# Two-stage attention block on one core: new order in the last head, loads before the last stores, and an output projection on four quarters of TensorE

## The reference

```
x = x + window_attention(group_norm(x))      # 49-pixel windows, 16 heads of 16, softmax
# second stage, on the result x1
n  = group_norm(x1)
p  = 25 shifted copies of n (5 x 5 neighbourhood, zeros outside)     # per pixel
q  = n
s  = sum over the 8 channels of a head of p * q                      # 8 heads, 25 scores per pixel
a  = softmax(s over the 25 shifts)
o  = sum over the 25 shifts of p * a                                 # 64 channels
out = x1 + w_out @ o + b_out                                         # w_out is 64 x 64
```

## Time and profile before

| | us |
|---|---|
| median of the runs | 1789.05 |
| the profiled execution, its time | 1798.7 |
| its span | 1797.0 |
| VectorE busy | 1434.3 (80%) |
| TensorE busy | 1435.7 (80%) |
| GpSimd busy | 1187.3 (66%) |
| ScalarE busy | 1051.5 (59%) |

### The profile page before, as it was taken

How to read it: one execution, slowest core, us unless ns; L and a number is a source line. 1 busy time by engine, 2 the same in 40 slices (tenths; PEclk the granted TensorE clock), 3 DMA queues, 4 the chain that set the end, 5 groups by cost and what they waited for, 6 DMA issues and landing times.

```text
span 1797.0 us, 60281 instructions
## 1 busy us (share of the span) xinstructions
PE 1435.7 (80%) x25001; PEld 704.2 (39%) x25001; DVE 1434.3 (80%) x1975; ACT 1051.5 (59%) x1883; POOL 1187.3 (66%) x860
## 2 busy tenths in 40 slices
PE   4999999999999999936887869777786876867745
PEld 2656666666666666610222212212221221213322
DVE  4776777777777777769999998999989899995924
ACT  3446777777777777735555747466574656543300
POOL 5334555555555555500999899999999999995700
PEclk9568999999999999956898998999999899997868
DMA  8702010202015101060225133252312422026079
GB/s 334 278 11 55 18 54 18 54 18 54 18 49 87 54 18 54 18 165 7 56 51 128 29 75 78 50 129 51 88 49 59 115 51 67 22 68 247 21 289 390
DMA packets 106860, 156.12 MB, mean 87 GB/s; under 512 B 71362, under 2 KB 83650, under 8 KB 100034
## 3 DMA queue, kind: packets, MB, share of 16 engines
q1 hardware_dynamic: 106690, 153.60, 29.2%
HBM read 81.92 MB, written 65.20 MB: 82 GB/s over the span
## 4 chain that ended last, share of the span: by engine, by line
PE 39%; POOL 27%; DVE 16%; issue 12%; ACT 2%; SPq 1%; DMA 1%; DVEq 0%; POOLq 0%
POOL arena L800 20%; PE PS L1312 6%; PE PS L1471 5%; PE PS L1321 5%; PE PS L1337 5%; POOL arena L811 4%; DVE arena L1104 4%; PE PS L1289 4%; DVE arena L1100 4%; PE PS L1281 4%; PE PS L1494 3%; PE PS L1300 2%; PE PS L1351 2%; DVE arena L1211 2%; PE PS L1419 2%
## 5 line engine op out<-in xcount | busy, mean ns | idle before, releaser
L800 POOL TENSOR_TENSOR arena<-arena 128x2016 f32<-128x2016 f32 (+2 forms) x168 | 604.9, 3635 | 78.9 <-PE PS L1419 78.7
L1211 DVE TENSOR_TENSOR arena<-arena,PS 128x1568 f32<-128x1568 f32 x348 | 610.3, 1778 | 39.6 <-PE PS L1471 32.6
L766 POOL TENSOR_TENSOR arena<-arena,consts 128x196 f32<-128x196 f32 x512 | 294.3, 608 | 278.1 <-ACT arena L850 278.1
L1471 PE MATMUL PS<-arena,consts 32*32 32x392 f32 x12800 | 391.3, 513 | 83.8 <-DVE arena L1211 46.9
L992 ACT ACTIVATE PS<-arena 128x392 f32<-128x392 f32 x348 | 172.9, 499 | 271.4 <-DVE arena L1211 269.5
L1419 PE MATMUL PS<-arena,consts 128*32 128x504 f32 (+2 forms) x1664 | 225.6, 618 | 119.9 <-POOL arena L800 76.7
L1471 PEld LDWEIGHTS PS<-arena,consts 32*32 32x32 f32 x12800 | 140.2, 104 | 337.4 <-DVE arena L1211 179.1
L1100 DVE TENSOR_REDUCE arena<-PS 128x8 f32<-128x392 f32 x256 | 143.3, 560 | 142.3 <-PE PS L1312 140.9
L875 ACT ACTIVATE arena<-PS 128x512 f32<-128x512 f32 x256 | 153.0, 598 | 155.0 <-PE PS L1321 151.6
L811 POOL TENSOR_TENSOR arena<-arena 128x1568 f32<-128x1568 f32 x52 | 159.3, 3076 | 49.0 <-ACT arena L938 21.6
L1321 PE MATMUL PS<-consts,arena 128*128 128x128 f32 x1024 | 176.6, 297 | 0.2
(11 more groups left out here) (105 smaller groups left out, 1670.6 us busy)
## 6 DMA issues: line engine op xcount, KB each, us to landing
arena<-x_wide_dram SPq DMA_DIRECT2D x256, 82.5 KB, 2.1
arena<-x_wide_dram SPq DMA_DIRECT2D x32, 660.0 KB, 8.3
x_wide_dram<-arena SPq DMA_DIRECT2D x12, 1125.0 KB
arena<-in_x_dram SPq DMA_DIRECT2D x8, 1568.0 KB, 15.2
x_wide_dram<-arena SPq DMA_DIRECT2D x64, 196.0 KB, 4.4
x_dram<-arena SPq DMA_DIRECT2D x8, 1568.0 KB, 7.4
attn_dram<-arena SPq DMA_DIRECT2D x256, 49.0 KB, 2.9
arena<-x_dram SPq DMA_DIRECT2D x8, 1568.0 KB, 18.9
```

What stands on the lines that cost most here:

```text
L766: i = nc.gpsimd.tensor_tensor(k_bd[k][:, r], keys.unsqueeze(1).to_broadcast([P, HEADS_T, S]), head_mask.unsqueeze(2).to_broadcast([P, HEAD ...
L800: nc.gpsimd.tensor_tensor(tile, x_part, by, ALU.mult).then_inc(pool_tile, 1)
L1211: nc.vector.tensor_tensor(by_channel(v_tiles[n % V_RING]), shifted_values(half, k), over_channels(PS[:, 2 + n % W_BANKS, 0:PIX]), ALU.mult ...
L1471: mm = nc.tensor.matmul(PS[dst, 4 + i, 0:PIX], ident[src, src], tile[src, c * PIX:(c + 1) * PIX], start=done == 0, stop=done == NK - 1)
```

## The change: what it does

1. `RECIPROCAL_LAST`: in the last head VectorE's reciprocal stands before the last 12 of its value products, not before the last 24.
2. `POOL_SHARE`: in the last head GpSimd makes 8 + 8 value products, not 7 + 10; VectorE 34, not 33. GpSimd's scale of half 0 stands before its last four products, not behind all.
3. In the planner the last value load counts as 24 us, not 40, and the early reload waits in the plan until head 6 is done. SP now issues the last value load ahead of the reloads, and ScalarE's normalisation of those pixels moves forward in its list.
4. The store of the last half is issued by ScalarE (`store_late_half`), the store of half 0 stays on SP and is issued when its scale is done.
5. The tiles of x1 get another layout: partition = half of the pixels (2) x channel (64), and both images of the pair lie one behind the other in a row. A reload of a pair, and an output store of a pair, is now two DMAs of 64 partitions with runs of 6272 B.
6. When all products are summed, SP issues the reload of pairs 6 and 7 and the load of the channels of heads 0 to 6 of pairs 0 to 5 (56 rows for each image), and only then waits for the last stores; the 8 missing rows of each image and the pairs 6 and 7 follow. Every load of `attn_dram` is split by image.
7. The projection runs as 64x64 blocks: rows (image) x columns (half of the pixels) give four blocks, 128 matmuls in all where there were 64. VectorE adds in two instructions of 784 columns where there was one of 1568.

```
-POOL_SHARE = [[(16, 18), (17, 21, 22)]] * (LH - 1) + [[range(18, NK), range(15, NK)]]
+POOL_SHARE = [[(16, 18), (17, 21, 22)]] * (LH - 1) + [[range(17, NK), range(17, NK)]]
+RECIPROCAL_LAST, SCALE_LAST = 12, 4
+HALF = HW // 2
+OLD = (LH - 1) * HD
+PARTED = 6
...
-            if n == len(own) - RECIPROCAL_AT:
+            if n == len(own) - (RECIPROCAL_AT if j < LH - 1 else RECIPROCAL_LAST):
...
-            order += [("scale", j - 2, 0), ("scale", j - 2, 1)] + own[0] + own[1] + [("scale", LH - 1, 0)]
+            order += [("scale", j - 2, 0), ("scale", j - 2, 1)] + own[0] + own[1][:SCALE_LAST] + [("scale", LH - 1, 0)] + own[1][SCALE_LAST:]
...
-                sp.dma_start(x1_in[bp], x1_dram[:, bp, :]).then_inc(x1_reloaded[bp], 16)
+                for half in range(2):
+                    dst = x1_in[bp][half * C:(half + 1) * C].rearrange("p (b n) -> p b n", b=2)
+                    sp.dma_start(dst, x1_halves[:, bp, :, half * HALF:(half + 1) * HALF]).then_inc(x1_reloaded[bp], 16)
...
+            def load_attn(bp, channels):
+                for b2 in range(2):
+                    rows = slice(b2 * C + channels.start, b2 * C + channels.stop)
+                    sp.dma_start(at_in[bp][rows], attn_rows[rows, bp, :]).then_inc(attn_loaded[bp], 16)
+
+            sp.wait_ge(v_summed, len(V_ORDER))
+            sp.wait_ge(ring_summed, len(RING_ORDER))
+            for bp in range(early_pairs, BP):
+                reload_x1(bp)
+            for half in range(2):
+                sp.wait_ge(o_stored[half], STORES * (LH - 1))
+            for bp in range(PARTED):
+                load_attn(bp, slice(0, OLD))
             for half in range(2):
                 sp.wait_ge(o_stored[half], STORES * LH)
-
             for bp in range(BP):
-                if bp >= early_pairs:
-                    reload_x1(bp)
-                sp.dma_start(at_in[bp], attn_rows[:, bp, :]).then_inc(attn_loaded[bp], 16)
+                load_attn(bp, slice(OLD if bp < PARTED else 0, C))
             for bp in range(BP):
                 sp.wait_ge(fin_ready, 2 * bp + 2)
-                sp.dma_start(out_rows[:, bp, :], x1_in[bp]).then_inc(out_stored, 16)
-            sp.wait_ge(out_stored, 16 * BP)
+                for half in range(2):
+                    src = x1_in[bp][half * C:(half + 1) * C].rearrange("p (b n) -> p b n", b=2)
+                    sp.dma_start(out_halves[:, bp, :, half * HALF:(half + 1) * HALF], src).then_inc(out_stored, 16)
...
+            def store_late_half():
+                act.wait_ge(out_norm, 1)
+                for i in range(GROUPS):
+                    b2, first = i * GROUP // C, i * GROUP % C
+                    for c in range(CH):
+                        dst = attn_dram[b2, LATE[0] * HD + LATE[1] * CH + c].rearrange("bp rg n -> (bp rg) n")
+                        nc.scalar.dma_start(dst[first:first + GROUP], o_loc[LATE[1]][c * GROUP:(c + 1) * GROUP, i]).then_inc(o_stored[LATE[1]], 16)
...
-                    for k in range(4 * g, 4 * g + 4):
-                        i = nc.tensor.matmul(PS[:, k, 0:PIX], wout_T, at_in[bp][:, k * PIX:(k + 1) * PIX],
-                                             start=True, stop=True)
+                    for n in range(2 * g, 2 * g + 2):
+                        for half in range(2):
+                            for b2 in range(2):
+                                rows = slice(b2 * C, (b2 + 1) * C)
+                                first = half * HALF + n * PIX
+                                i = nc.tensor.matmul(PS[half * C:(half + 1) * C, 4 * b2 + n, 0:PIX], wout_T[rows, rows],
+                                                     at_in[bp][rows, first:first + PIX], start=True, stop=True)
```

More of the change, by code:

```diff
@@ L101 @@
 SHARE_AT = [[9, 13], [18, 21, 24]]
-POOL_SHARE = [[(16, 18), (17, 21, 22)]] * (LH - 1) + [[range(18, NK), range(15, NK)]]
+POOL_SHARE = [[(16, 18), (17, 21, 22)]] * (LH - 1) + [[range(17, NK), range(17, NK)]]
 LATE = (LH - 1, 1)
+HALF = HW // 2
+OLD = (LH - 1) * HD
+PARTED = 6
+LAST_LOAD = ("v",) + LATE
 def shape_of(t):
@@ L264, in merge_orders @@
                 free + [("pixels", kind, j, a, piece - 1) if piece else None],
-                0.3 if piece else LOADING if free else FIRST_LOADS[kind, j])
+                0.3 if piece else (LOADING if (kind, j, a) != LAST_LOAD else 24.0) if free else FIRST_LOADS[kind, j])
     end, free = {}, {eng: 0.0 for eng in todo}
@@ L291, in merge_orders @@
     sync.append((max(end[("score", LH - 1, S_TILES - 1, 1)], end[("total", LH - 2, NK - 1)],
-                     end[("weight", V_AT[("value", LH - 1, 0, 0)] - 1)]),
+                     end[("weight", V_AT[("value", LH - 1, 0, 0)] - 1)],
+                     max(end[s] for s in V_ORDER + RING_ORDER if s[:2] == ("value", LH - 2)) + 0.01),
                  ("reload",)))
@@ L309, in build @@
     x_rows = x.rearrange("(bp b2) c h w -> (b2 c) bp (h w)", b2=2)
-    out_rows = out.rearrange("(bp b2) c h w -> (b2 c) bp (h w)", b2=2)
+    out_halves = out.rearrange("(bp b2) c h w -> c bp b2 (h w)", b2=2)
+    x1_halves = x1_dram.rearrange("(b2 c) bp n -> c bp b2 n", b2=2)
     attn_rows = attn_dram.rearrange("b2 c bp rg n -> (b2 c) bp (rg n)")
@@ L627, in store_half @@
             def store_half(j, half):
[L628 to L631, removed]
+                sp.wait_ge(out_scaled, 2 * j + half + 1)
                 for i in range(GROUPS):
@@ L687, in _ @@
                 elif step[0] == "store":
-                    store_half(step[1], step[2])
+                    if step[1:] != LATE:
+                        store_half(step[1], step[2])
                 else:
                     reload_early()
+            def load_attn(bp, channels):
[10 more added lines that the diff above has]
+                load_attn(bp, slice(0, OLD))
             for half in range(2):
@@ L694, in _ @@
             for bp in range(BP):
-                if bp >= early_pairs:
-                    reload_x1(bp)
-                sp.dma_start(at_in[bp], attn_rows[:, bp, :]).then_inc(attn_loaded[bp], 16)
+                load_attn(bp, slice(OLD if bp < PARTED else 0, C))
             for bp in range(BP):
                 sp.wait_ge(fin_ready, 2 * bp + 2)
-                sp.dma_start(out_rows[:, bp, :], x1_in[bp]).then_inc(out_stored, 16)
-            sp.wait_ge(out_stored, 16 * BP)
+                for half in range(2):
+                    src = x1_in[bp][half * C:(half + 1) * C].rearrange("p (b n) -> p b n", b=2)
+                    sp.dma_start(out_halves[:, bp, :, half * HALF:(half + 1) * HALF], src).then_inc(out_stored, 16)
+            sp.wait_ge(out_stored, 32 * BP)
         @block.gpsimd
@@ L1021, in _ @@
                     evict_half(*step[1:])
+            store_late_half()
         @block.vector
@@ L1241, in _ @@
             for bp in range(BP):
-                dve.wait_ge(x1_reloaded[bp], 16)
+                dve.wait_ge(x1_reloaded[bp], 32)
                 for g in range(2):
                     dve.wait_ge(fproj, 2 * bp + g + 1)
[L1245 to L1248, removed]
+                    for b2 in range(2):
+                        first = b2 * HALF + 2 * g * PIX
+                        part = x1_in[bp][:, first:first + 2 * PIX].rearrange("p (k n) -> p k n", k=2)
+                        i = nc.vector.scalar_tensor_tensor(out=part, in0=PS[:, 4 * b2 + 2 * g:4 * b2 + 2 * g + 2, 0:PIX],
+                                                           scalar=par[:, 4:5], in1=part, op0=ALU.add, op1=ALU.add)
+                    i.then_inc(fin_ready, 1)
         @block.tensor
@@ L1488, in _ @@
             for bp in range(BP):
-                pe.wait_ge(attn_loaded[bp], 16)
+                pe.wait_ge(attn_loaded[bp], 64 if bp < PARTED else 32)
                 for g in range(2):
```

## The result

The changed kernel takes 1852.09 us (median of 4 runs, 1845.53 to 1855.95), the kernel before beside it 1796.56. The ratio is 1.03 with a 95% interval of 1.0222 to 1.0377: slower, by 40 to 68 us. The forecast was +48 us, or 1837 us: the measured time lies 15 us above it, at the very top of the range of 1764 to 1852, and about half of the 15 us is the kernel before, whose median is 1796.56 here where the forecast started from 1789. The profiled executions differ by 53.3 us in their spans, 1850.3 against 1797.0.

A forecast was written before the change was run, and what follows sets the result against it. The DMA engines were taken to close the kernel: last sum at 1713.3 plus an end of 131.8 us gave 1845.1 against 1797.0, +48 us; carried to 1789, that made 1837 us, range 1764 to 1852.

The forecast's parts named there:

- The rate of loads: Reloads and attention-result loads into 64 partitions: taken at 208 GB/s, where 128 partitions move 424 to 427.
- The last sum: End of the last head: all summed at 1713.3 us, where it was 1707.05; bounds 1698 and 1726.
- the 7.2 us for one packet of TensorE's instructions: Last head, during reloads: TensorE gets four sums' instructions per 7.2 us, so 24 of 50 sums by 1672.
- The bound of 10 us: Last head: if a packet of instructions takes 10 us instead of 7.2, all is summed at 1726.
- The chain behind it: Last head: reciprocal at about 1680, spread landed 1695.8, GpSimd's scale to 1698.8, four products to 1711.3, last sums 2 us.
- Rival D: Chance 0.05: 64 partitions no limit, GpSimd doesn't wait for the spread, uneven transfers cost nothing; -39 us, 1750 us.
- The stores from ScalarE: After the norm: 16 issues, 9 us with landing, hidden behind SP's transfers; uncovered it would cost 11 us.
- The uneven transfers: Loads at the end: 8 rows occupy 8 engines at most, 56 rows put four on some; up to 4 us.
- The end: After the last sum: ten pairs in 77.2 us, eight out 49.4, start and stop 5.2; together 131.8 us.
- rival B: Chance 0.20: loads at half rate, outputs near full rate, or engines drifting apart; end 112.5 us, span 1825.8, +29, 1818 us.
- 5.2 for starting and stopping: End of the kernel: of 73.0 us for 28.98 MB, 5.2 us go to starting and stopping transfers.
- TensorE and VectorE: Projection: four blocks side by side cut TensorE's 45 us to some 23; VectorE's adds of 1.04 us stay hidden.

The follow-up runs named there:

- the two cuts of the kernel before: Kernel before, each x1 reload and attention-result load cut in two DMAs: by partitions, ratio 1.0244; by columns, ratio 1.0005.
- the kernel with the scale last: GpSimd's half-0 scale behind all products: on the kernel before with the change's head and late reloads during last stores, 1778.63 us (3.42 wait); on the change, 1847.3 (23 earlier).
- the kernel with cut stores: Kernel before, every output store cut in two DMAs of 64 partitions, loads untouched: ratio 1.0006.

## Why the prediction was right, step by step

**The rate of loads** carried the forecast, and it held: 208 GB/s taken, 217 to 221 measured, and the two cuts of the kernel before separate the partitions from the length of the runs and the number of DMAs. The last early reload had landed at 1672.9, as forecast with 1672.

**The last sum** was put at 1713.3 and came at 1724.2. The mis-sized term is the 7.2 us for one packet of TensorE's instructions: with the DMA engines full of 64-partition loads it is 9.15, and the 24 sums that the forecast put into this stretch are six packets, so 11.7 us more. The bound of 10 us had been named with 1726. The reciprocal came at 1691.8 instead of 1680. The chain behind it was right: 33 us from the reciprocal's start to the last sum predicted, 32.4 measured, with GpSimd waiting 14.33 us for the spread where "some 15" stood. Rival D, in which GpSimd does not wait, was not what happened, but it was nearly what could be had: in the kernel with the scale last GpSimd waits 3.42 us.

**The stores from ScalarE** were costed at nothing, hidden behind SP's transfers, and so it was, although the chain that ended last runs through their landing. That landing took 28.37 us, but the transfers issued before kept the DMA engines busy (share 0.92 from 1740 to 1760, 0.97 to 1780), and the missing rows would have stood behind them in any case: in the kernel with the scale last they were requested 23 us earlier and landed 3.5 us earlier. The landing grows with what else is queued: 1.69 us with nothing, 4.27 and 6.71 with two reloads of 128 partitions, 10.93 with the same reloads on 64 partitions, 15.76 and 28.37 with the early loads too. That is six kernels of this study. In the kernels that start their loads only after the stores, it is waited for in full.

**The uneven transfers** were the step that was furthest off, "up to 4 us" in the range and nothing in the sum. The forecast saw that 8 rows occupy 8 engines at most, and took 56 rows to be spread unevenly, where they ran on 14 engines. Above all it did not see that the loads beside them slow down as well. From 1783 to 1806 all transfers together moved 2.75 MB in 23 us, and at 221 GB/s that would be 12.4: 10.6 us lost, an estimate. How much of it is the few engines and how much the few partitions they write was not tried.

**The end** was summed to 131.8 us and took 126.1, and that it came so near is luck: two errors nearly cancel. The outputs ran at 387 instead of 260 GB/s: 33 us instead of 49.4, close to the 30.1 of rival B. With 5.2 for starting and stopping that leaves 88 us for the loads, where 77.2 stood, and the 10.6 us of the slow stretch are about this difference; the rest of the loads ran somewhat faster than 208, which about pays for the 0.8 MB of stores. With the outputs right and all else as it stood, the forecast would have been rival B's 1825.8 for the span, 24.5 us too low.

**TensorE and VectorE**: 27.2 us busy for the projection (23 predicted), 1.024 us for an add (1.04 predicted). Both steps hold, and both were worth nothing, since neither engine was the bound of that stretch. Part of the 27.2 is the clock: after its 68.6 us of waiting TensorE's first 32 records ran at a granted clock of 0.50, the lower of its two levels, and took 5.55 us, where later ones at 1.00 take 1.55 us for 16.

In sum: +10.9 for the last sum, -5.7 for the end, and so +53 where +48 was forecast.

## What to carry to other kernels

Where the DMA share is 1, ask first what a change does to the bytes a second of a transfer, and only then what it does to the engines: here a layout made for TensorE halved the rate of all loads, and 36 us of the end were lost to save 18 us of an engine that was not the bound. If a load has to be cut, cut it by columns (ratio 1.0005 here) and not by partitions (1.0244), and write it so that its slowest dimension is a multiple of 16 on both sides. Work that needs nothing belongs ahead of a step that waits, in each engine's own list: four products moved ahead of one scale were worth 11 us of the last head.

## What the runs showed of the hardware

- A load into 64 partitions moves 217 to 221 GB/s with all DMA engines busy, whatever its runs (6272 or 12544 B). A store out of 64 partitions moves 389 GB/s in the change (1820 to 1840 us) and 398 in the kernel with cut stores (1760 to 1780), both with nothing but outputs under way. The forecast had 260 for it.
- A transfer runs on as many DMA engines as its shape allows: 16 for 64 rows, 14 for 56, 8 for 8 by their landing steps, and 2 where the source was written 2 x 64 x 1568, with 53 GB/s at share 0.13.
- Transfers of 8 rows and loads of 64 rows side by side moved 120 GB/s for 23 us at a share of 0.94: a high share does not tell that the bytes flow.
- TensorE got the instructions of four sums every 9.15 us beside 64-partition reloads and every 6.2 to 7.2 us beside 128-partition ones, and paused for them; with the DMA engines at a share of 0.14 there was no such pause.
